# A gated attention and mixture block: tile addresses, whole-row operands, the first products by blocks, and DMA transposes of two batches

## The reference, cut to what matters

```python
q  = round_fp8(layernorm(x))        # scaled per token and per block of 128 features
c  = round_fp8(ctx)                 # scaled per 128x128 block, one 256x256 matrix per batch
x1 = x + tanh(g_xattn) * einsum('emk,enk->emn', q, c)
h  = layernorm(x1)
probs = softmax(h @ gate_w.T)       # 8 experts; the 4 best, renormalised: comb
moe   = sum_e comb[e] * (silu(h @ wg[e].T) * (h @ wu[e].T)) @ wd[e].T     # 176 wide
sh    = (silu(h @ swg.T) * (h @ swu.T)) @ swd.T                           # 704 wide
out   = x1 + tanh(g_ffn) * (moe + sigmoid(h @ shared_gate_w.T) * sh)
```

## Time and profile before

| | |
|---|---|
| median of the runs | 189.81 us |
| the profiled execution: its time, its span | 189.74 us, 187.9 us |
| busy: PE, PE weight loads | 162.2 us (86%), 123.6 us (66%) |
| busy: DVE, ACT, POOL | 130.6 us (69%), 101.3 us (54%), 77.8 us (41%) |
| mean granted TensorE clock | 0.997 |

### The profile page before, as it was taken

One profiled execution on the slowest core, in us unless ns is written; L12 is line 12 of the kernel. 1 busy time (PEld: TensorE's weight loads), 2 busy tenths in 40 slices (PEclk: granted clock), 3 DMA queues, 4 the chain that ended last, 5 costly groups with the idle time before them and its releaser, 6 DMA issues.

```text
span 187.9 us, 2355 instructions
## 1 busy us (share of the span) xinstructions
PE 162.2 (86%) x714; PEld 123.6 (66%) x715; DVE 130.6 (69%) x280; ACT 101.3 (54%) x217; POOL 77.8 (41%) x90
## 2 busy tenths in 40 slices
PE   0023298999999999999999999999999999999992
PEld 0011144787886687667788878878768888888870
DVE  0799996384878999999988845862478545554553
ACT  2449333278777885546665553595553455445430
POOL 3220325044865454443465433444444654544410
PEclk9999999999999999999999999999999999999998
DMA  4599700000289995222332332502999100000003
GB/s 135 178 405 400 307 2 0 0 3 2 64 228 234 326 400 178 85 58 84 84 87 84 84 84 85 195 5 62 230 240 329 67 2 0 0 0 0 0 0 115
DMA packets 11057, 22.75 MB, mean 121 GB/s; under 512 B 1938, under 2 KB 2194, under 8 KB 11044
## 3 DMA queue, kind: packets, MB, share of 16 engines
q1 hardware_dynamic: 10612, 21.94, 37.9%
q10 hardware_dynamic: 432, 0.66, 1.3%
HBM read 21.51 MB, written 1.09 MB: 120 GB/s over the span
## 4 chain that ended last, share of the span: by engine, by line
PE 73%; DVE 16%; issue 3%; DMA 3%; ACT 1%; POOL 1%; DVEq 1%; ACTq 0%; POOLq 0%
PE bank L988 47%; PE bank L1077 6%; PE bank L1078 6%; PE bank L1081 6%; DMA cw<-ctx_t 3%; DVE bank L760 1%; DVE deq_x L660 1%; PE bank L969 1%; DVE x L677 1%; DVE xq L653 1%; DVE silu L745 1%; PE bank L1017 1%; DVE xc L652 1%; POOL rstd L281 1%; DVE amax_c L570 1%
## 5 line engine op out<-in xcount | busy, mean ns | idle before, releaser
L287 POOL TENSOR_TENSOR w_lo<-w_raw,w_hi 128x512 fp32r<-128x512 f32 (+1 forms) x34 | 42.8, 1258 | 61.4 <-ACT w_hi L416 60.6
L988 PE MATMUL bank<-h_hi,w_hi 128*128 128x512 f32 x132 | 53.8, 408 | 0.7 <-DVE bank L756 0.4
L988 PE MATMUL bank<-h_lo,w_hi 128*128 128x512 f32 x132 | 52.2, 395 | 0.0
L988 PE MATMUL bank<-h_hi,w_lo 128*128 128x512 f32 x132 | 52.1, 395 | 0.0
L437 ACT ACTIVATE a_hi<-bank 128x512 fp32r<-128x512 f32 (+1 forms) x34 | 20.3, 598 | 38.7 <-DVE bank L760 38.1
L293 POOL TENSOR_TENSOR w_lo<-w_raw,w_hi 128x256 fp32r<-128x256 f32 (+1 forms) x34 | 26.0, 765 | 19.5 <-ACT w_hi L420 19.4
L760 DVE TENSOR_TENSOR bank<-silu,bank 128x512 f32<-128x512 f32 x32 | 22.2, 695 | 15.1 <-PE bank L988 13.2
L988 PEld LDWEIGHTS bank<-h_hi,w_hi 128*128 128x128 f32 x132 | 24.8, 188 | 8.2 <-issue 3.1
L769 DVE TENSOR_TENSOR a_lo<-bank,a_hi 128x512 fp32r<-128x512 f32 x32 | 22.1, 689 | 11.5 <-ACT a_hi L437 11.3
L988 PEld LDWEIGHTS bank<-h_hi,w_lo 128*128 128x128 f32 x132 | 24.8, 188 | 6.0
L988 PEld LDWEIGHTS bank<-h_lo,w_hi 128*128 128x128 f32 x132 | 24.8, 188 | 4.9
(11 more groups left out here) (108 smaller groups left out, 173.6 us busy)
## 6 DMA issues: line engine op xcount, KB each, us to landing
w_raw<-w_full SPq DMA_DIRECT2D x32, 384.0 KB, 7.4
mix_b<-rows_dram SPq DMA_DIRECT2D x8, 256.0 KB, 6.5
out_t<-fin SPq DMA_DIRECT2D x4, 256.0 KB, 2.1
mix_b<-rows_dram SPq DMA_DIRECT2D x4, 224.0 KB, 6.2
x<-xs SPq DMA_DIRECT2D x3, 256.0 KB, 7.2
mix_b<-rows_dram SPq DMA_DIRECT2D x4, 192.0 KB, 5.9
mix_b<-rows_dram SPq DMA_DIRECT2D x4, 160.0 KB, 5.9
cw<-ctx_t ACTq DMA_DIRECT2D x2, 256.0 KB, 5.5
```

The lines of the kernel that those rows point to most:

```text
L287: nc.gpsimd.tensor_tensor(w_lo[:, n % 2, 0:cols], w_raw[:, n % RING, 0:cols], w_hi[:, n % 2, 0:cols].bitcast(F32), ALU.subtract).then_inc( ...
L988: last = nc.tensor.matmul(out, w[k][a], x_of[k][b], start=(start and k == 0 and i == 0), stop=(stop and k == blocks - 1 and i == 2))
```

## The change

- **Tile addresses.** mix_b, sg_b, w_raw, w_hi, w_lo, silu, a_hi, a_lo and fin are allocated ahead of the small tiles.
- **Whole rows.** blk_w has 128 rows (zeroed by POOL); lg_rows has 128 rows and is transposed with `eye`, DVE adds the two parts of the logits (`lg_low`), and fold goes; the short unit's low matmuls use all 128 rows. Its gate writes the UP bank, and the next gate doesn't wait for its product.
- **First loads.** x and the context of batches 0 and 1 come in halves, one from SP and one from ACT, in the order x(0), ctx(0), x(1), ctx(1).
- **First products.** The transposes of y2(1), its h_hi and h_lo go by blocks of 128 features into two banks, router(0) and gate(0) are woven together by blocks, and the logits' transposes stand between the two blocks of up(0).
- **POOL.** low_gate_w no longer waits for the tokens of batch 1; low_gu(0) waits for the quantised context of batch 1. Four more clock fillers stand ahead of attend(1).
- **DMA transposes.** For batches 2 and 3, SP issues four DMA transposes each from xq to xqt; PE's transposes and ACT's copies of them go. attend(2) stands behind up(11), and residual0(2) behind high_a(11).
- **Order in down.** OUT[0] gets its last pass before OUT[1] gets its second.

```diff
-        blk_w = sb("blk_w", [CB, HALVES, P])
+        blk_w = sb("blk_w", [P, HALVES, P])
-        lg_rows = sb("lg_rows", [2 * GP, HN])
+        lg_rows = sb("lg_rows", [P, HN])
...
+            def transpose_xq(b):
+                sp.wait_ge(xq_ready, b + 1)
+                for jj, j in enumerate(tiles(b)):
+                    for k in range(KC):
+                        sp.dma_start(xqt[:, b, k, jj * P:(jj + 1) * P], xq[:, j, k, :], transpose=True).then_inc(xqt_landed[b - HB], 16)
...
-            sp.dma_start(x[:, 0:1, :], xs[:, 0:1, :]).then_inc(x_landed[0], 16)
-            load_x(1)
+            for b in range(HB):
+                sp.dma_start(x[:, BT * b:BT * b + 1, :], xs[:, BT * b:BT * b + 1, :]).then_inc(x_landed[b], 16)
+                sp.dma_start(cw[:, b, 0], ctx_t[:, b, 0]).then_inc(ctx_landed[b], 16)
...
-            for n in range(RING, RING + UNITS + 1):
+            for n in range(RING, RING + 9):
+                load_w(n)
+            transpose_xq(2)
+            load_w(RING + 9)
+            transpose_xq(3)
+            for n in range(RING + 10, RING + UNITS + 1):
                 load_w(n)
...
             roots(1)
-            pool.wait_ge(xq_ready, 2)
             low_gate_w()
+            pool.wait_ge(cq_ready[1], 1)
             low_gu(0)
...
-            a.dma_start(x[:, 1:BT, :], xs[:, 1:BT, :]).then_inc(x_landed[0], 16)
             for b in range(HB):
-                a.dma_start(cw[:, b], ctx_t[:, b]).then_inc(ctx_landed[b], 16)
+                a.dma_start(x[:, BT * b + 1:BT * (b + 1), :], xs[:, BT * b + 1:BT * (b + 1), :]).then_inc(x_landed[b], 16)
+                a.dma_start(cw[:, b, 1], ctx_t[:, b, 1]).then_inc(ctx_landed[b], 16)
...
+            def high_h_by_blocks(b):
+                ts = slice(b * S, (b + 1) * S)
+                for k, done in enumerate((h_hi_first, h_hi_done)):
+                    a.wait_ge(y2t_psum, KC * b + k + 1)
+                    nc.scalar.activation(h_hi[:, k, ts], Y2T1[k][:, 0:S], ACT.Copy).then_inc(done, 1)
...
+            high_a(11)
             residual0(2)
-            high_a(11)
...
-                nc.vector.tensor_copy(lg[:], LOGIT_T[h][:, 0:HT * GP].rearrange("p (j g) -> p j g", j=HT)).then_inc(lg_ready, 1)
+                parts = LOGIT_T[h][:].rearrange("p (j r) -> p j r", j=HT)
+                after(did(nc.vector.tensor_copy(lg_low[:], parts[:, :, GP:2 * GP])))
+                nc.vector.tensor_tensor(lg[:], parts[:, :, 0:GP], lg_low[:], ALU.add).then_inc(lg_ready, 1)
...
+            def first_products():
+
+                pe.wait_ge(gate_split, 1)
+                pe.wait_ge(gu_lo_done, 1)
+                pe.wait_ge(x1t_copied, 2)
+                pe.wait_ge(h_hi_done, 1)
+                pe.wait_ge(h_hi_first, 1)
+                w = w_gu(0, 0)
+                for k in range(KC):
+                    if k == 1:
+                        pe.wait_ge(h_hi_done, 2)
+                    nc.tensor.matmul(LOGIT[0][:], gate_hl[:, k, :], h_hi[:, k, 0:HN], start=(k == 0), stop=False)
+                    nc.tensor.matmul(GATE[:], w[k][0], h_hi[:, k, 0:HN], start=(k == 0), stop=False)
+                    nc.tensor.matmul(GATE[:], w[k][1], h_hi[:, k, 0:HN], start=False, stop=False)
+                pe.wait_ge(h_lo_done, HB)
+                for k in range(KC):
+                    last = nc.tensor.matmul(LOGIT[0][:], gate_hl[:, k, :], h_lo[:, k, 0:HN], start=False, stop=(k == KC - 1))
+                last.then_inc(logits_ready, 1)
+                for k in range(KC):
+                    last = nc.tensor.matmul(GATE[:], w[k][0], h_lo[:, k, 0:HN], start=False, stop=(k == KC - 1))
+                last.then_inc(gate_done, 1)
...
-                    last = nc.tensor.matmul(LOGIT_T[h][:, jj * GP:(jj + 1) * GP], lg_rows[:, jj * P:(jj + 1) * P], fold[:],
-                                            start=True, stop=True)
+                    last = nc.tensor.transpose(LOGIT_T[h][:, jj * P:(jj + 1) * P], lg_rows[:, jj * P:(jj + 1) * P], eye[:])
...
-                    elif was == SHORT:
-                        pe.wait_ge(act_done, n)
-                    else:
+                    elif was > SHORT:
                         pe.wait_ge(mixed_done, mixes(n - 1))
-                three_passes(GATE[:], w_gu(n, 0), tokens(h), True, True).then_inc(gate_done, 1)
+                three_passes(UP[n % 2][:] if i == SHORT else GATE[:], w_gu(n, 0), tokens(h), True, True).then_inc(gate_done, 1)
...
-                        nc.tensor.matmul(OUT[k][:], w_lo[0:LAST, n % 2, cols[k]], a_hi[0:LAST, n % 2, :],
-                                         start=False, stop=stop).then_inc(out_done, 1)
+                        nc.tensor.matmul(OUT[k][:], w_lo[:, n % 2, cols[k]], a_hi[:, n % 2, :], start=False, stop=stop)\
+                            .then_inc(out_done, 1)
...
+            keep_clock_up(4)
             attend(1)
...
-            router(0)
-            gate(0)
+            first_products()
+            w = w_gu(0, 1)
+            three_passes(UP[0][:], w[:1], tokens(0)[:1], True, False)
             transpose_logits(0)
-            up(0)
+            three_passes(UP[0][:], w[1:], tokens(0)[1:], False, True).then_inc(up_done, 1)
...
             gate(11)
+            up(11)
             attend(2)
-            up(11)
             down(10)
```

More of the change, by code:

```diff
@@ L68, in flamingo_gated_block @@
         h_lo = sb("h_lo", [P, KC, T], F32R)
+        mix_b = sb("mix_b", [P, MOE, HN])
+        sg_b = sb("sg_b", [P, HN])
+        w_raw = sb("w_raw", [P, RING, WC])
+        w_hi = sb("w_hi", [P, 2, WC], F32R)
+        w_lo = sb("w_lo", [P, 2, WC], F32R)
+        silu = sb("silu", [P, 2, HN])
+        a_hi = sb("a_hi", [P, 2, HN], F32R)
+        a_lo = sb("a_lo", [P, 2, HN], F32R)
+        fin = sb("fin", [P, 2, HN])
         bn = sb("bn", [P, 2, TILES, 6])
@@ L106, in flamingo_gated_block @@
         comb_rows = sb("comb_rows", [G, HN])
[L107 to L116, removed]
         eye = sb("eye", [P, P])
         eye_b = sb("eye_b", [P, P], BF16)
-        fold = sb("fold", [2 * GP, GP])
         bank = [stack.enter_context(nc.psum_tensor(f"bank{i}", [P, HN], F32)) for i in range(8)]
@@ L144, in flamingo_gated_block @@
         mix_landed = [sem(f"mix_landed{c}") for c in range(MOE)]
+        xqt_landed = [sem(f"xqt_landed{b}") for b in range(HB, B)]
         stored = sem("stored")
@@ L290, in low_d @@
             def low_d(n):
[L291 removed]
+                at = GUL if n % UNITS == SHORT else GU
                 pool.wait_ge(d_hi_done, n + 1)
[L293 to L294 removed]
+                nc.gpsimd.tensor_tensor(w_lo[:, n % 2, GU:WC], w_raw[:, n % RING, at:at + D],
+                                        w_hi[:, n % 2, GU:WC].bitcast(F32), ALU.subtract).then_inc(d_lo_done, 1)
             def low_gate_w():
@@ L470, in _ @@
             high_h(0)
-            high_h(1)
+            high_h_by_blocks(1)
             copy_logits(0)
@@ L506, in _ @@
             high_a(8)
-            front(9)
-            middle(9)
-            copy_xqt(2)
-            high_a(9)
+            unit(9)
             front(10)
             middle(10)
-            copy_xqt(3)
             high_a(10)
@@ L982, in transpose_y2, with transpose_y2_by_blocks @@
                 transpose_tokens(b, y2, Y2T, y2t_psum)
+            def transpose_y2_by_blocks(b):
+                pe.wait_ge(y2_ready, b + 1)
+                pe.wait_ge(x1t_copied, 1)
+                for k in range(KC):
+                    for jj, j in enumerate(tiles(b)):
+                        last = nc.tensor.transpose(Y2T1[k][:, jj * P:(jj + 1) * P], y2[:, j, k * P:(k + 1) * P], eye[:])
+                    last.then_inc(y2t_psum, 1)
             def three_passes(out, w, x_of, start, stop):
@@ L994, in tokens, with w_gu @@
                 return [(h_hi[:, k, ts], h_lo[:, k, ts]) for k in range(KC)]
+            def w_gu(n, which):
+                at = which * KC * P
+                return [(w_hi[:, n % 2, at + k * P:at + (k + 1) * P], w_lo[:, n % 2, at + k * P:at + (k + 1) * P])
+                        for k in range(KC)]
             def router(h):
-                pe.wait_ge(gate_split, 1)
                 pe.wait_ge(h_hi_done, HB * (h + 1))
-                if h == 0:
-                    pe.wait_ge(x1t_copied, 2)
-                else:
-                    pe.wait_ge(h_lo_done, HB * h + 1)
+                pe.wait_ge(h_lo_done, HB * h + 1)
                 ts = slice(h * HN, (h + 1) * HN)
@@ L1025, in transpose_comb @@
                 last.then_inc(comb_psum, 1)
-            def w_gu(n, which):
-                at = which * KC * P
-                return [(w_hi[:, n % 2, at + k * P:at + (k + 1) * P], w_lo[:, n % 2, at + k * P:at + (k + 1) * P])
-                        for k in range(KC)]
             def keep_clock_up(count):
```

92 lines of the change are left out of this document (47 added, 45 removed).

## The result

The changed kernel takes 185.54 us (185.42 to 185.58, 4 runs) against 189.80 (189.59 to 190.03, 4 runs) for the kernel before; ratio 0.9774, 95% interval 0.9757 to 0.9791. The forecast was 185.7. The profiled execution took 185.51 us for a span of 183.7, so 4.2 us came off the span, for a forecast of 4.05. The total agrees better than its terms do: the tile addresses, taken as worth nothing, gave 1.9 us, and the other terms together fell short by 1.7.

A forecast was written before the change was run, and what follows sets the result against it. DVE was taken to bound 0 to 31 and 58.5 to 92 us, PE 33 to 57 and 92.5 to 182. Terms -1.1 - 1.4 + 0.45 + 0 - 2.0 = -4.05 gave 185.7 us; 8-in-10 range 183.0 to 188.3.

The forecast's parts named there:

- The rule drawn from it for the third stretch: 58.5 to 92 us: PE edits count nothing, as PE would only arrive earlier at the same DVE result.
- Front, -1.1: First 31 us: 0.4 us from earlier loads plus 0.7 net from POOL's new order, which frees the deq_x pair.
- First products and logits(0), -1.4: First half: 0.7 us from weaving router and gate(0) by blocks, 0.74 from whole-row logits transposes.
- route, +0.45: Ahead of gate(3): later logits transposes and longer route_compare delay acts(0) and silu(2); loss 0.45 us, bounds 0.1 and 0.8.
- Gate(13), -2.05: End of DVE's stretch: gate(13) starts about 2 us earlier, from front, first products and logits less the route's loss.
- it waits for mixed as before: Gate(7) to gate(13) wait for DVE's mixed product as before, so PE and ACT savings there count 0.
- the third rival: DVE takes back more: POOL collisions fall elsewhere, loads come no earlier, route costs 0.8; 187.2 us, chance 15%.
- Short unit, x transposes, DMA transposes in the first half: 0: 57 to 82 us: savings on PE and ACT lie under DVE's 98% row, and DMA transposes are hidden; worth 0.
- Second half, -2.0: PE-bound end: logits 0.74, short unit 0.77, gate(23) stall 0.35, less 0.1, tail 0.23; together 2.0 us.
- +0.1 at gate(25): Second half: loss of 0.1 us, as acts(24) on DVE becomes the later one at gate(25).
- Alignment, 0: Large tiles move from 32 to 0 modulo 64 bytes; taken as worth 0.
- the second rival: Alignment speeds up weight loads, 0.016 us off each matmul PE paces, 7.5 us; time 178, chance 10%.

The follow-up runs named there:

- experiment 7: Changed kernel with low weight parts of units 4 to 12 computed for 8 columns of each half only, POOL nearly idle: 179.69 us, ratio 0.9436.
- Experiment 10: Changed kernel with POOL's front order taken back: gate_hl and low_gu(0) both wait for xq of batch 1: 187.10 us.
- experiment 1: Kernel before with only the tile order changed, mix_b to fin allocated right behind h_lo: 189.85 us against 190.29, ratio 0.9978.
- experiment 5: Changed kernel with PE transposes and ACT copies for batches 2 and 3 in place of the DMA transposes: 185.80 us.
- experiment 11: Changed kernel with 64 rows again in the short unit's low down product and logits folded by eight small matmuls again: 187.85 us.
- experiment 8: Changed kernel with the two add_shared(1, k) moved two units later, into units 25 and 26: 185.56 us.
- experiment 2: Changed kernel with padding that puts its nine large tiles at 32 modulo 64 bytes: 187.33 us, ratio to before 0.9847.
- experiment 3: Changed kernel with only w_hi and w_lo at 32 modulo 64 bytes: 188.26 us.
- experiment 4: Changed kernel with only silu, a_hi and a_lo at 32 modulo 64 bytes: 187.61 us.
- experiment 9: Changed kernel rearranged so POOL's weight splitting and DVE's instructions without PSUM operand fall at different times, nothing left out: 180.57 us, ratio 0.9482.
- experiment 12: The rearranged kernel of experiment 9 with padding that puts the large tiles at 32 modulo 64 bytes: 182.65 us.
- experiment 6: Changed kernel with DVE's order in units 7 to 10 altered: exponent and magic instructions behind gated(n), rounding behind low_a(n): 185.69 us.

## Why the prediction was right, and where it was not

- **What bounds it.** Right in its places: DVE until 31 us, PE to 57, DVE to 90, PE to the end. But DVE's full row in the third stretch was not all work: 6.2 of 33.8 us went with POOL's splitting (experiment 7), and then PE was the bound there. The rule drawn from it for the third stretch, that an edit on PE is worth nothing there, was too kind: a faster PE moved ACT's and POOL's work against DVE's and cost about 1 us.
- **Front, -1.1.** Measured -1.7: 0.8 from the loads where I took 0.4 (the upper bound), of which 0.4 is a landing that varies; 1.06 from deq_x as taken; collisions elsewhere 0.13 for 0.35, since on gate_hl it was POOL that was held (0.78 us for 0.34), not DVE. Experiment 10 shows the net of POOL's new order, 0.93; the loads were not taken back in any run, and rest on the timelines.
- **First products and logits(0), -1.4; route, +0.45.** Measured -1.38 and +0.40, read from the timelines; no run takes the weaving by blocks back by itself.
- **Gate(13), -2.05.** Measured -1.42. Failed step: "it waits for mixed as before". Experiments 1 and 7 show what came instead, three instructions on POOL's lock. This is the mechanism of the third rival, at 1.05 us between acts(4) and gate(13); it had 15%, and no row of the sum carried it. Part of the better front is in that -1.42: at gate(3) 2.70 had arrived for 2.05.
- **Short unit, x transposes, DMA transposes in the first half: 0.** Right: experiment 5 for the transposes; gate(6) came 3.58 us earlier than before and gate(7) only 2.39; and in experiment 11 gate(7) is 0.39 late net of the landing, just what gate(3) was.
- **Second half, -2.0.** The terms logits 0.74, short unit 0.77, stall at gate(23) and tail 0.23 stand (0.71 and 0.81 in experiment 11; fin starts at 179.79 after an idle 0.69, for 0.92). The +0.1 at gate(25) was mis-sized: 0.95. I had priced acts(24) and left out that the add_shared pair, two SBUF inputs each, stands behind POOL's splitting; with PE earlier the pair went from 1.78 to 2.51 us, and each add takes 0.75 alone (experiment 8).
- **Alignment, 0.** Wrong: 1.9 us in total (experiment 2). It is the second rival's cause at 5 ns on average instead of its 16. Its argument ran over the weight loads, which still take 188 ns; and the argument against it, that h_hi at 0 streams no faster than a_hi at 32, fails because the other operand was off in both cases (experiments 3 and 4).

Without the alignment the changed kernel would have taken 187.3 (experiment 2; 186.9 if its ratio is put to this result's 189.80), 1.2 to 1.6 above the forecast. In that kernel gate(13) is 1.20 us earlier than before's, for 2.05, and the rest 1.1 shorter, for 2.0. The forecast's 185.7 is right by luck: two misses of the same size cancelled.

## What to carry to other kernels

A busy row near 100% may hold waiting: compare an instruction's longest duration with its shortest before calling its engine the bound, and count the excess over the stretch (here 6.2 of 33.8 us, the difference that experiment 7 made). Where DVE and POOL both work all the time, give POOL the time in which DVE reads PSUM and let it wait out the rest; that was worth 5 us here, more than the whole change. And a gain on one engine that runs ahead of a bound stretch isn't worth nothing but anything between both signs, until the phases behind it are checked.

## What the runs showed of the hardware

- Matmuls of 128x512 f32 were 227.4 ns apart with both operands at a multiple of 64 bytes, about 233 with one of them at 32 modulo 64 (experiments 3 and 4) and 230 with both (down matmuls of experiment 2), for unchanged load durations of 188 ns.
- In the profiled executions of experiments 3, 8, 10 and 11 the granted clock fell to half for 3.4 us, between 0.3 us before gate(7) and 0.4 us after it, behind waits of PE of 0.3 to 0.5 us and then 1.1 (0.6 in experiment 11). Other runs of the same programs kept a mean clock of 1.00, and the changed kernel's trace has the same waits, 0.54 and 1.12, without the fall. No run of experiments 7, 9 and 12, where PE waits there for 0.7 us at most, had a mean clock below 0.996.
- Eight 128x128 bf16 DMA transposes out of one queue occupied it for 1.25 us each and landed 2.3 us after issue, in the median.
- A DVE instruction of 128x512 with two SBUF inputs took 1.76 us beside POOL's splitting for 0.68 (experiment 6), one of 128x4 1.28 for 0.22; those with an input from PSUM kept 0.68 to 0.70.
